# The loop over two of four chunks written out, in a five-engine kernel for a Mamba-like mixer, attention and two feed-forward layers

## The reference

```python
x = L0_attn_a_x                                    # (8, 512, 128)
x = x + mixer(layernorm(x))                        # state recurrence over t, 8 heads, state 64 x 128
x = x + layernorm(x) @ ternary(weight).T * alpha + bias
x = x + attention(layernorm(x))                    # over the first axis (8), 16 heads of 8
x = x + layernorm(x) @ ternary(weight).T * alpha + bias

# mixer, per time step
h = alpha_t * h + beta_t * Bx_prev + gamma_t * Bx_t    # Bx_t = u_t (x) rope(B_t)
y_t = h . rope(C_t);   y = rmsnorm(y) @ out_proj_w.T
```

## Time and profile before

| | |
|---|---|
| median of 3 runs | 612.39 us (611.85 to 613.84) |
| the profiled execution | 614.66 us, of which 612.9 us lie between the first and the last instruction |
| instructions in the profile | 13462 |
| mean granted TensorE clock | 0.961 of full speed |
| busy: PE, PEld, DVE, ACT, POOL | 86%, 72%, 77%, 79%, 68% |
| chunk 0, first scan | 44.8 us |
| the loop's code is first executed | about 138 us |
| second execution of the loop's body | about 275 us |
| chunk 3 begins | about 413 us |

### The profile page before, as it was taken

The page is one execution under the profiler, slowest core; times in us unless marked ns, Lnnn a source line. Parts: engine busy times, 40 slices in busy tenths (PEclk is TensorE's granted clock), DMA queues, the critical chain, the costliest instruction groups (busy, mean ns, idle before and its releaser), DMA issues.

```text
span 612.9 us, 13462 instructions
## 1 busy us (share of the span) xinstructions
PE 528.9 (86%) x3960; PEld 441.5 (72%) x3960; DVE 470.5 (77%) x1085; ACT 482.2 (79%) x1478; POOL 415.5 (68%) x548
## 2 busy tenths in 40 slices
PE   4978999999999898897999898899988888878177
PEld 4857888888787777786887777688767666666166
DVE  6765666686669999976669999986669999732985
ACT  3799999999988888797988879699988898642001
POOL 7358778877768877785768877786776867422421
PEclk9989999999999998998999999999999999977688
DMA  8741221223201111212200111323111111100001
GB/s 203 210 124 39 73 96 57 75 82 101 67 25 38 59 57 58 94 60 73 75 30 36 59 58 59 90 62 93 59 57 59 53 50 52 35 18 1 0 1 35
DMA packets 52324, 39.43 MB, mean 64 GB/s; under 512 B 7317, under 2 KB 48026, under 8 KB 52250
## 3 DMA queue, kind: packets, MB, share of 16 engines
q1 hardware_dynamic: 44858, 34.86, 18.8%
q10 hardware_dynamic: 7392, 3.67, 2.1%
HBM read 33.44 MB, written 4.46 MB: 62 GB/s over the span
## 4 chain that ended last, share of the span: by engine, by line
PE 31%; DVE 29%; ACT 20%; issue 13%; POOL 3%; DMA 2%; DVEq 1%; ACTq 0%; POOLq 0%; SPq 0%
ACT turned L856 6%; ACT turned L871 6%; PE ps L1513 5%; DVE lmat L1182 4%; DVE area L1289 3%; PE ps L1682 3%; PE ps L1650 3%; ACT area L925 3%; PE ps L1840 3%; DVE state L1221 2%; PE ps L1736 2%; PE ps L1745 2%; DVE area L1276 2%; DVE mmat L1190 2%; DVE area L1272 2%
## 5 line engine op out<-in xcount | busy, mean ns | idle before, releaser
L871 ACT ACTIVATE turned<-ps,sct 128x128 f32<-128x128 f32 x376 | 110.6, 447 | 0.0
L856 ACT ACTIVATE turned<-ps,sct 128x128 f32<-128x128 f32 x368 | 103.1, 439 | 5.4 <-DMA sct<-packed 3.9
L1182 DVE TENSOR_TENSOR_SCAN lmat<-arow,band 128x512 f32<-128x512 f32 x64 | 84.2, 1320 | 6.1 <-POOL band L625 6.1
L604 POOL TENSOR_TENSOR cn<-turned 128x256 f32<-128x256 f32 x64 | 55.6, 869 | 47.0 <-ACT turned L871 47.0
L1190 DVE TENSOR_TENSOR mmat<-ps,lmat 128x512 f32<-128x512 f32 x64 | 43.9, 686 | 45.3 <-PE ps L1650 45.0
L762 ACT ACTIVATE area<-ps 128x256 f32<-128x256 f32 (+1 forms) x68 | 35.3, 580 | 55.1 <-PE ps L1840 26.6
L1650 PE MATMUL ps<-cT,bT 128*128 128x128 f32 x512 | 69.8, 280 | 8.6 <-DVE state L1221 5.9
L1650 PEld LDWEIGHTS ps<-cT,bT 128*128 128x128 f32 x512 | 63.7, 193 | 15.8 <-issue 14.6
L604 POOL TENSOR_TENSOR bn<-turned 128x256 f32<-128x256 f32 x64 | 52.3, 817 | 32.0 <-PE ps L1682 22.5
L1555 PE MATMUL ps<-w_sel_hi,xt_hi 128*128 128x512 f32 x128 | 59.7, 467 | 0.3 <-ACT turned L871 0.3
L1682 PE MATMUL ps<-wu,bn 128*128 128x128 f32 x384 | 54.5, 286 | 3.5 <-DVE mmat L1190 3.4
(11 more groups left out here) (238 smaller groups left out, 1420.3 us busy)
## 6 DMA issues: line engine op xcount, KB each, us to landing
arow<-alpha_rows SPq DMA_DIRECT2D x32, 512.0 KB, 3.6
drow<-decay_rows SPq DMA_DIRECT2D x64, 128.0 KB, 3.0
area<-in_L_attn_a_x_dram SPq DMA_DIRECT2D x4, 512.0 KB, 6.2
xT_rows<-turned SPq DMA_DIRECT2D x4, 512.0 KB, 5.3
xt<-xT_rows SPq DMA_DIRECT2D x32, 64.0 KB, 2.5
area<-in_L_attn_a_x_dram ACTq DMA_DIRECT2D x8, 256.0 KB, 2.9
out_dram<-area ACTq DMA_DIRECT2D x6, 256.0 KB, 2.4
area<-L_attn_a_sel_proj_w_dram SPq DMA_DIRECT2D x2, 512.0 KB, 6.4
```

The lines of the kernel that those rows point to most:

```text
L604: pool.tensor_tensor(out[:, 0], zc[:, 0], zs[:, 1], ALU.subtract)
L856: last = act.activation(dst[h][:, N * q:N * q + N], bank(BK_B)[:, N * q:N * q + N], ACT.Copy, scale=scalars(c, k)[:, at + HH * h + q:at + ...
L871: last = act.activation(dst[h][:, N * q:N * q + N], bank(BK_C)[:, N * q:N * q + N], ACT.Copy, scale=scalars(c, k)[:, at + HH * h + q:at + ...
L1182: dve.tensor_tensor_scan(lmat[h], arow[i2][:, HH * P * h:HH * P * (h + 1)], band[h], 0.0, ALU.mult, ALU.add).then_inc(l_dve, 1)
```

## The change

In `run_chunks` (for PE, DVE, ACT and POOL) and in SP's list of loads the sequencer's loop becomes a loop of Python. `c` is then the number 1 or 2, the body stands in the program twice, and every count and address is a constant. The order of the work is kept.

```diff
@@ run_chunks
-    with eng.Fori(1, NC - 1) as c:
+    for c in range(1, NC - 1):
         for k in range(UNITS):
             step(c, k, pieces)
@@ SP
-            with sp.Fori(1, NC - 1) as c:
+            for c in range(1, NC - 1):
                 for b in range(NB):
                     tile_loads(c, b)
```

## The result

The changed kernel takes 608.18 us (606.79 to 610.11, 6 runs), beside 613.39 us (611.85 to 615.45, 6 runs) for the kernel before in the same series: a ratio of 0.9916, 95% interval 0.9891 to 0.9942. It is faster by 5.2 us, near the forecast sum of 5.6. The forecast median was 606.8 us, worked out from 612.39 for the kernel before; that kernel's own median moved up by 1.0 us in this series, and the rest of the 1.4 us is the smaller gain. The profiled execution took 609.03 us with a span of 607.3 us; 609.0 and 607.3 were forecast.

What follows compares the result with a forecast made beforehand. No engine was full; the loop's backward branch was taken to stall PE and ACT at the chunk 1 to 2 border. 5.28 + 0.24 + 0.3 - 0.2 = 5.62 us less, from 612.39 to 606.8 us, range 604.4 to 609.6.

Steps and rivals of the forecast that it cites:

- The backward branch: Border of chunks 1 to 2: removing the once-taken branch saves 5.28 us, 3.72 of stall plus 1.56; bounds 3.7 to 5.3.
- The clock: PE from L1663 to the scores behind the branch: 1.56 us longer, partly at the lower clock after PE's idle time.
- Entering the loop: Loop entry, from bn's transposes to the scores: 0.24 us saved, mostly behind ACT's first table load; bounds 0.17 to 1.28.
- The register instructions: Both loop rounds: removing them saves 0.3 us, at 0.12 us per exposed place; bounds 0 to 1.2.
- The table load: Moved ahead of ACT's first exponential, which comes 0.65 us later; costs 0.2 us, bounds 0 to 0.65.
- Part of the gain is lost again: Rival: PE's clock falls elsewhere or chunk 2 waits more for sct loads; 3.1 us gained, 609.3 us; chance 0.14.
- More than counted: Rival: register counts slowed every unit in both rounds, 6.2 us on top, 600.6 us; chance 0.10.
- Fetch falls behind in straight code: Rival: written-out code misses fetches; one miss about 612.1 us (0.07, shared with no effect), two 617.4 (two or more 0.03).
- The edit does nothing: Rival: all engines' stall at the border lies beside another wait, so no change; chance 0.07, shared with one fetch miss.

Runs made afterwards that it cites:

- e3: Changed kernel with chunks 1 and 2 each in a sequencer loop of one round, backward branch never taken; 610.06 us, ratio 0.9934 to the kernel before.
- e4: Changed kernel plus a two-round loop around one fulfilled wait between chunks 1 and 2 on four engines; 609.22 us, ratio 0.992 to the kernel before.
- e8: Changed kernel plus six two-round loops on ACT between chunks 1 and 2, bodies of about 50 to 600 instructions, mostly fulfilled waits; 876.13 us.
- e10: Kernel before with PE alone written out; ACT, DVE, POOL and SP keep the loop; ratio 0.9977 to the kernel before.
- e5: Changed kernel with the loop kept on PE alone, other engines written out; ratio 0.9973 to the kernel before.
- e7: Changed kernel with the loop kept on DVE and POOL, other engines written out; ratio 0.9932 to the kernel before.
- e1: The changed kernel run and profiled once more, no edit; 607.61 us, ratio 0.9888 to the kernel before.
- e6: Changed kernel with the loop kept on ACT alone, other engines written out; ratio 0.9976 to the kernel before.

## Why the prediction was right

*The backward branch, 3.72 + 1.56 = 5.28 us.* Measured 5.28 on PE (11.53 to 6.25) and 5.25 on DVE's scans, and the gain is kept in chunk 2. e3 shows that it is the branch taken backwards and not the loop's frame, e4 and e8 that it is the distance, and the branches of the packed trace that each engine stands at its own. The size came out right from a description with a hole in it: DVE too stood at its own branch, idle for 2.54 us, which the prediction left out; it had DVE wait for PE. In the rows the idle time carries POOL's name. The sum came out because the written-out border to chunk 3, from which it was read, had none of the three stalls. Had the edit been made on PE alone, the same pricing would have promised 3.7 us or more, and e10 gave 2.5 at the border and no sure gain in the whole.

*The clock, 1.56 us in it.* Right for this border: 1.00 in place of 0.66. e5 to e7 show the cause as far as it can be shown here: a lone stall of PE (3.43 us) or a wait of 2.3 to 2.9 us is followed by the lower clock; without a gap (changed kernel, e1, e3, e4) it doesn't fall there. It isn't certain in a single execution: in e10 PE waits 2.35 us and the clock stays at 1.00, so the 1.56 us can be smaller.

*Entering the loop, 0.24.* In the changed kernel bn to scores at the entry is 147.61 - 140.56 = 7.05 us, against 7.35: 0.30. On the scans it is 0.29: from that at 137.53 to that at 149.74 it is 12.21 us, in the changed kernel 11.92. It hangs on ACT, as forecast: 12.20 to 12.23 us in e3, e6 and e10, which have ACT's table load at the first chunk's head, 11.98 in e5 and 11.93 in e7, which don't.

*The register instructions, 0.3.* SP's sct load is issued 0.08 us behind the update of state (277.97, and 277.04 + 0.85), as forecast. On ACT the waits for sct in the middle of the chunks are 0.09 to 0.11 us shorter (1.14 and 1.15 before, 1.05 and 1.04 after), so the price of 0.12 for an exposed place was about right. The profile calls the idle time after the edit issue, not a wait for the DMA. On the scans the 0.3 is about half: 0.10 us ahead of the exponential and 0.03 in the last unit of each chunk. The 16.37 us of the unit late in chunk 2 are not theirs: the same unit takes 15.69 us in e10, where ACT, DVE and POOL keep their register instructions, and 15.69 in e5, where PE keeps them.

*The table load, -0.2.* The exponential came 1.31 us behind the end of u_nat's copy (198.53 to 199.84) instead of 0.65, 0.66 later as forecast. The scans around it lost 0.30 us, while the interval ahead of them was 0.10 shorter: 18.59 us against 18.39 over both intervals, which is the 0.2, and DVE waits 0.21 us for the exponential. The drain of about 1380 ns that the Trainium skill adds to a load (ScalarE: Activation LUTs, What ACT_TABLE_LOAD costs) isn't to be seen: the row gives 1.28 us, and the exponential starts 0.01 us behind its end.

*The rivals.* "Part of the gain is lost again" happened by size in the single execution (1.4 us more in code that didn't change), but for the most part by chance of the clock (the stretch around 480 us) and not through sct: the waits for sct at the chunk's head are 0.43 and 0.47 us and hold up no scan at the border. "More than counted" did not come: rows two and four of the ledger keep 0.14 us in all, once the two places that are not the edit's are left out. "Fetch falls behind in straight code" did not come: the longest idle time of PE that the trace calls issue stays at 1.67 us, near 521 us, as before (near 526); on ACT it is 1.83 us in chunk 3, at an instruction that in the two profiles of the kernel before waited 0.24 and 2.19 us. "The edit does nothing" can't be excluded for PE written out alone: e10's interval reaches 1.0004.

## What to carry to other kernels

Where a hardware loop's border stands in a kernel next to written-out code for the same work, lay the two over each other on an engine that does one thing per unit; the difference is the price, clock included. Here a loop body of 438 instructions or more paid at its turn on each engine that had one, at the same time, and a body of 246 did not. An engine of the chain that stays in the loop brings its stall back, so an edit is judged with all of them written out: PE alone gained nothing clear of the noise, PE, ACT and SP together came to 0.9932 and all five to 0.9916, 0.9888 and 0.9904 in three runs. Where the profile names a releaser whose work ends just then, look whether the order is the same in a kernel without the loop. Before a difference of under 3 us between two profiles is explained, look up where each had its stretches of lower clock.

## What the runs showed of the hardware that was not expected

- From a backward branch to the loop's head it takes 3.6 to 3.9 us on PE, 3.0 to 3.3 on ACT (516 instructions back), 2.8 to 2.9 on DVE (438), 0.3 on POOL (246) and SP (123), and 0.2 for a body of a few instructions (e4). The idle times in the rows are shorter (PE 3.4 to 3.7, ACT 2.5 to 2.7, DVE 2.5 to 2.6), because earlier work still runs when the branch is reached (DVE's L1261 until 272.53, with the branch at 271.93). On ACT the step lies between 300 and 400 instructions, 0.27 and 2.75 us. The Trainium skill (Runtime: NRT & Kernel Launch, Instruction fetch mechanics) has the kind of wait; the sizes and the step are from these runs.
- A stall at a branch can bear another engine's name: DVE's 2.54 to 2.59 us read as a wait for POOL's band in four profiles, where e5 and e6, with DVE written out, have none.
- The granted clock falls at places that differ between executions of one program, and the same program took 0.8 us more with such a stretch around 375 us (last scan of chunk 2 118.53 us behind the border in e1, 117.69 in the first profile), and 1.6 to 2.9 more with one around 480 us.
